# A transformer-like block on one core: three LayerNorms folded into weights and later scales, the sine product moved to VectorE, new orders

## The reference

```
ln(x)  = (x - mean(x)) / sqrt(var(x) + 1e-5)            # per row
1: q,k,v = ln(x) @ Wqkv.T ; q,k = elu(q)+1, elu(k)+1     # 16 heads of 8, linear attention
   x += ((q @ (k.T v)) / (q . sum(k) + 1e-6)) @ Wproj.T + bproj
2: y  = relu(ln(x) @ W_fc.T)**2 @ W_proj.T               # 128 -> 512 -> 128
   x += (spikes counted over 5 steps of mem = 0.9*mem + y - (mem>1)) / 5
3: Q,K,V = ln(x) @ Wq.T, Wk.T, Wv.T ; Q,K rotated by cos, sin of the row number
   x += softmax(Q K.T / sqrt(128), keys up to row+1) @ V
4: as 2, with the same weights
```

## Time and profile before

| what | value |
|---|---|
| median of 3 runs | 205.46 us (203.21 to 206.3) |
| the profiled execution | 205.26 us |
| its span, first to last instruction | 203.5 us |
| mean granted TensorE clock | 0.98 |
| busy: TensorE, VectorE, ScalarE, GpSimd | 180.9, 159.6, 114.2, 64.0 us |
| chain that ended last, by engine | TensorE 72%, VectorE 12%, issue 7%, ScalarE 3%, GpSimd 3% |

### The profile page before, as it was taken

One profiled execution on the slowest core, in us unless ns is written; L12 is line 12 of the kernel. 1 busy time (PEld: TensorE's weight loads), 2 busy tenths in 40 slices (PEclk: granted clock), 3 DMA queues, 4 the chain that ended last, 5 costly groups with the idle time before them and its releaser, 6 DMA issues.

```text
span 203.5 us, 3973 instructions
## 1 busy us (share of the span) xinstructions
PE 180.9 (89%) x1264; PEld 159.5 (78%) x1264; DVE 159.6 (78%) x495; ACT 114.2 (56%) x265; POOL 64.0 (31%) x86
## 2 busy tenths in 40 slices
PE   7389969799989989598969999799999999999971
PEld 2189948597787868586868999699999999999961
DVE  2995685999897999988998787955879663974895
ACT  2269831659649188287836786364064945574260
POOL 7760054353372834232752105400010213012110
PEclk9969996999999999999999999999999999999998
DMA  5980000000000030300000000000000001000111
GB/s 179 279 252 2 3 0 0 2 3 0 0 5 2 1 102 4 89 14 3 4 0 0 0 3 0 0 2 3 0 3 0 2 3 52 2 0 3 52 52 52
DMA packets 9825, 5.96 MB, mean 29 GB/s; under 512 B 447, under 2 KB 9422, under 8 KB 9806
## 3 DMA queue, kind: packets, MB, share of 16 engines
q1 hardware_dynamic: 9086, 5.25, 8.7%
q10 hardware_dynamic: 720, 0.47, 0.8%
HBM read 4.66 MB, written 1.05 MB: 28 GB/s over the span
## 4 chain that ended last, share of the span: by engine, by line
PE 72%; DVE 12%; issue 7%; ACT 3%; POOL 3%; DMA 1%; DVEq 0%; ACTq 0%; POOLq 0%
PE bank_o L1099 14%; PE bank_m L1026 10%; PE bank_p L1087 7%; PE bank_s L910 6%; PE bank_s L912 5%; PE bank_s L911 5%; PE bank_h L910 3%; DVE xn L712 3%; PE bank_h L912 3%; PE bank_h L911 3%; PE bank_m L927 3%; PE bank_p L1062 2%; PE bank_h L962 2%; POOL rstd L457 2%; DMA id_sb<-in_ident 1%
## 5 line engine op out<-in xcount | busy, mean ns | idle before, releaser
L1099 PE MATMUL bank_o<-vone,pt 128*128 128x128 f32 x272 | 35.7, 275 | 0.9 <-DVE pt L845 0.5
L1099 PEld LDWEIGHTS bank_o<-vone,pt 128*128 128x128 f32 x272 | 33.6, 191 | 2.3 <-DVE pt L845 0.9
L1026 PE MATMUL bank_m<-wd,hid 128*128 128x128 f32 x256 | 32.9, 276 | 1.0 <-ACT hid L623 1.0
L1026 PEld LDWEIGHTS bank_m<-wd,hid 128*128 128x128 f32 x256 | 31.1, 192 | 2.2 <-issue 1.4
L612 ACT ACTIVATE relu<-bank_h 128x512 f32<-128x512 f32 (+2 forms) x44 | 20.5, 483 | 15.6 <-PE bank_h L912 12.7
L450 POOL TENSOR_SCALAR veps<-mom 128x4 f32<-128x4 f32 (+2 forms) x19 | 4.4, 231 | 62.9 <-DVE mom L694 62.8
L499 POOL TENSOR_TENSOR hid<-relu 128x512 f32<-128x512 f32 (+2 forms) x14 | 12.4, 892 | 37.0 <-ACT relu L612 37.0
L672 ACT COPY pt<-bank_p 128x512 f32<-128x512 f32 (+3 forms) x25 | 13.2, 528 | 16.2 <-PE bank_p L1087 13.8
L794 DVE SCALAR_TENSOR_TENSOR spiked<-y,spiked 128x512 bf16<-128x512 f32 (+2 forms) x34 | 19.1, 562 | 0.6
L712 DVE TENSOR_SCALAR xn<-xs,mom,rstd 128x128 f32<-128x128 f32 x54 | 17.2, 377 | 3.0 <-POOL rstd L457 2.8
L457 POOL TENSOR_TENSOR rstd<-veps,mhalf 128x4 f32<-128x4 f32 (+2 forms) x19 | 18.4, 966 | 1.4 <-POOL veps L450 0.2
(11 more groups left out here) (137 smaller groups left out, 426.5 us busy)
## 6 DMA issues: line engine op xcount, KB each, us to landing
xs<-in_x SPq DMA_DIRECT2D x4, 256.0 KB, 5.2
cos_sb<-in_cos SPq DMA_DIRECT2D x4, 256.0 KB, 4.8
sin_sb<-in_sin SPq DMA_DIRECT2D x4, 256.0 KB, 5.2
out_x<-xs SPq DMA_DIRECT2D x3, 256.0 KB, 2.3
mask_sb<-in_mask SPq DMA_DIRECT2D x1, 320.0 KB, 8.3
...
```

Source lines behind the costliest of these rows:

```text
L1026: last = nc.tensor.matmul(MB[:, C * t:C * t + C], hid[:, j % 2, m, P * t:P * t + P], wd[:, m, :], start=(m == 0), stop=(m == M - 1))
L1099: last = nc.tensor.matmul(O[:, C * (i % TG):C * (i % TG) + C], pt[:, n % 3, P * b:P * b + P], v[:, k, :], start=(k == 0), stop=(k == i))
```

## The change

LayerNorms 2 to 4 (step index 1 to 3) no longer normalise the rows ahead of the product. Since a product with ln(x) equals rstd times the product of x with weights whose mean over the input channels has been taken off, the change does this:

- The weights W_fc and the rotary Wq, Wk, Wv are centred once: `centre` on GpSimd makes the identity minus 1/128, and the steps `centre-1` and `centre-2` on TensorE multiply it with the raw weights in full precision, 512 columns into H1 and 384 into MB. `w_hi-1`, `w_hi-2` (ScalarE) and `w_lo-1`, `w_lo-2` (both on VectorE now) read these banks; `w_hi-1` also copies the centred W_fc back to w_fc_sb.
- `turn-n-g` for n of 1 to 3 transposes the raw rows xs; it waits for the residual sum that made them (rows_ready) and not for `norm`. `norm-n-g` for these n and `nmr` are gone. `stats` and `rstd` stay.
- For LayerNorm 3 the rstd is applied to q, k and v when the bank is copied (`qkv_copy`: an activation with the scale taken from the table). For LayerNorms 2 and 4, relu and square carry the scale through as its square, so `rstd` holds 1 / (var + eps) there (power -1) and `y` applies it: one activation for each tile on ScalarE, or one product with a broadcast operand on VectorE.
- The sine product moves from GpSimd to VectorE; `rsin` and its use are the same.
- All four orders are new: which engine squares, copies and evacuates which piece changes, w_lo-0 comes after rstd-0-1 on GpSimd, kv-0-0 comes between the first two turns.

```diff
     "pe": """
+turn-0-0 kv-0-0 turn-0-1 kv-0-1 q-0 kv-1-0 kv-1-1 turn-0-2 q-1 acc-0 turn-0-3 kv-2-0 kv-2-1 q-2 kv-3-0 kv-3-1 acc-1
+q-3 acc-2 acc-3 centre-1 ao-0 centre-2 ao-1 at-0 pr-0 at-1 turn-1-0 ao-2 f1-0-0 turn-1-1 f1-0-1 pr-1 f1-0-2 f1-0-3
+at-2 f1-1-0 f1-1-1 f2-0-0 f2-0-1 pr-2 turn-1-2 f1-1-2 f1-1-3 ao-3 turn-1-3 f1-2-0 f1-2-1 f2-1-0 f1-2-2 f1-2-3 f2-1-1
...
+turn-3-4 pv-15-0 f2-8-0 f1-9-0 f2-8-1 f1-9-1 pt-15-3 pv-15-1 pv-15-2 pv-15-3 f1-9-2 f1-9-3 turn-3-5 f1-10-0 f1-10-1
 f2-9-0 f1-10-2 f1-10-3 f2-10-0
     "act": """
+q_exp-2 kv_exp-3-0 kv_exp-3-1 q_exp-3 w_hi-1 w_hi-2 aT_copy-0 hi-1-0 aT_copy-1 relu-0-0 hi-1-1 relu-0-1 sq-0-0 sq-0-1
...
     "dve": """
+heads-1 w_lo-2 x1-0 stats-1-0 lo-1-0 heads-2 lo-1-1 x1-1 sq-0-2 stats-1-1 stats-1-2 y-0 spike-0-0 spike-0-1 x1-2
     "pool": """
-vnext_zero ids rstd-0-0 w_lo-0 rstd-0-1 rstd-0-2 bias-0 rstd-0-3 w_lo-2 bias-1 bias-2 rstd-1-0 nmr-1-0 rstd-1-1 sq-0-1
+vnext_zero ids centre rstd-0-0 rstd-0-1 w_lo-0 rstd-0-2 bias-0 rstd-0-3 rstd-1-0 bias-1 bias-2 sq-1-1 rstd-1-1
...
+        def make_sin(eng, g):
+            eng.wait_ge(v_ready, TG * (g + 1))
+            eng.wait_ge(trig_in[g], 32)
+            if g:
+                eng.wait_ge(half_ready[0], g)
+                eng.wait_ge(half_ready[1], g)
+            eng.tensor_tensor(
+                rsin[:].rearrange("p t (a c) -> p t a c", a=2),
+                qk[:, g % 2].rearrange("p t (a c) -> p t a c", a=2),
+                sin_sb[:, g % 2].unsqueeze(2).to_broadcast([P, TG, 2, C]), ALU.mult).then_inc(*one(done["sin", g]))
+
+        def rows_ready(eng, n, g):
+            t0, nt = NORM_JOBS[n][g]
+            if n == 0:
+                eng.wait_ge(x_in[g], 16)
+            elif n == 1:
+                eng.wait_ge(x1_ready, (t0 + nt - 1) // TG + 1)
+            elif n == 2:
+                eng.wait_ge(xf_ready, next(k for k, (a, b) in enumerate(JOBS) if a + b >= t0 + nt) + 1)
+            else:
+                eng.wait_ge(x3_ready, t0 + nt)
...
-                    nc.gpsimd.tensor_tensor(rstd[:, n, ts], veps[:, n, ts], mhalf[:, 0:nt],
+                    nc.gpsimd.tensor_tensor(rstd[:, n, ts], veps[:, n, ts], (mone if n % 2 else mhalf)[:, 0:nt],
...
+                elif step[0] == "centre":
+                    pool.wait_ge(id_in, 16)
+                    nc.gpsimd.tensor_scalar(centre[:], id_sb[:], -1.0 / C, None, ALU.add).then_inc(centre_ready, 1)
...
+                        act.wait_ge(centred[k], 1)
+                        src = (None, H1, MB)[k][:, 0:n]
+                    if k == 1:
+                        nc.scalar.copy(w_fc_sb[:], src)
+                    nc.scalar.copy(wh[:, o:o + n], src).then_inc(w_hi, 1)
...
-                    nc.scalar.copy(y[:, j % 2, 0:width], MB[:, 0:width]).then_inc(*one(done["y", j]))
+                    n, g, scale = scale_of(j)
+                    act.wait_ge(rstd_ready[n], g + 1)
+                    for t in range(JOBS[j][1]):
+                        last = nc.scalar.activation(y[:, j % 2, P * t:P * t + P], MB[:, P * t:P * t + P], ACT.Copy,
+                                                    scale=scale[:, t:t + 1])
...
-                    nc.scalar.copy(qk[:, g % 2, t, :], bank[:, 0:2 * C])
-                    nc.scalar.copy(v[:, n, :], bank[:, 2 * C:3 * C]).then_inc(v_ready, 1)
+                    scale = rstd[:, 2, n:n + 1]
+                    nc.scalar.activation(qk[:, g % 2, t, :], bank[:, 0:2 * C], ACT.Copy, scale=scale)
+                    nc.scalar.activation(v[:, n, :], bank[:, 2 * C:3 * C], ACT.Copy, scale=scale).then_inc(v_ready, 1)
...
-                    nc.vector.tensor_copy(y[:, j % 2, 0:width], MB[:, 0:width]).then_inc(*one(done["y", j]))
+                    nc.vector.tensor_tensor(
+                        y[:, j % 2, 0:width].rearrange("p (t c) -> p t c", c=C),
+                        MB[:, 0:width].rearrange("p (t c) -> p t c", c=C),
+                        scale.unsqueeze(2).to_broadcast([P, JOBS[j][1], C]), ALU.mult).then_inc(*one(done["y", j]))
...
+                if step[0] == "centre":
+                    k = step[1]
+                    bank = (None, H1, MB)[k]
...
+                    nc.tensor.matmul(bank[:, 0:WEIGHTS[k][1]], centre[:], RAW[k], start=True, stop=True).then_inc(
+                        centred[k], 1)
...
-                    pe.wait_ge(*done["norm", n, g])
+                    if n == 0:
+                        pe.wait_ge(*done["norm", n, g])
+                    else:
+                        rows_ready(pe, n, g)
...
+                        last = nc.tensor.transpose(bank[:, C * t:C * t + C], xs[:, t0 + t, :] if n else xn[:, j % 2, t, :],
+                                                   id_sb[:])
```

More of the change, by code:

```diff
@@ new lines @@
+at-3 f1-3-0 f2-2-0 f2-2-1 f2-2-2 count-0 f2-2-3 count-1 pr-3 turn-2-0 f1-3-1 f1-3-2 turn-1-4 qkv-0-0 f1-3-3 qkv-0-1
+qkv-0-2 f1-4-0 qkv-0-3 f2-3-0 f2-3-1 f2-3-2 f2-3-3 count-2 f1-4-1 tqk-0-0 tqk-0-1 turn-2-1 f1-4-2 f1-4-3 s-0-0 s-1-0
+qkv-1-0 qkv-1-1 qkv-1-2 pt-0-0 qkv-1-3 f2-4-0 f2-4-1 pt-1-0 f2-4-2 f2-4-3 count-3 pv-0-0 s-2-0 tqk-1-0 tqk-1-1
+turn-2-2 pv-1-0 pt-2-0 s-3-0 s-3-1 pv-2-0 s-4-0 pt-3-0 s-4-1 s-5-0 pv-3-0 qkv-2-0 pt-4-0 turn-3-0 s-5-1 qkv-2-1
+count-4 qkv-2-2 qkv-2-3 pt-4-1 turn-2-3 pv-4-0 pv-4-1 f1-5-0 pt-5-0 pt-5-1 s-6-0 f1-5-1 s-6-1 tqk-2-0 tqk-2-1 pv-5-0
@@ L187 @@
+rstd-1-2 sq-1-2 sq-1-3 lo-1-3 bias-3 rstd-1-3 rstd-2-0 sq-3-1 sq-3-2 rstd-1-4 rstd-2-1 sq-4-2 lo-2-2 rstd-2-2 lo-3-0
+rstd-3-0 sq-5-3 rstd-2-3 rot-3-1 rstd-3-1 sq-6-1 sq-6-0 rstd-3-2 sq-8-2 rstd-3-3 rstd-3-4 sq-10-1 rstd-3-5
 """,
@@ L223, in hybrid_block @@
         rstd = sb("rstd", 4, T)
-        nmean = sb("nmean", 4, T)
-        nmr = sb("nmr", 4, T)
         mhalf = sb("mhalf", TG)
-        xn = [sb(f"xn{k}", 2, TG, C) for k in range(2)]
+        mone = sb("mone", TG)
+        xn = sb("xn", 2, TG, C)
+        centre = sb("centre", P)
         xh = [sb(f"xh{k}", 2, W, dt=F32R) for k in range(2)]
@@ L363, in one @@
             return signal[0], 1
-        def on_act_before(norm, g):
-            return sum(engine_of["norm", norm, k] == "act" for k in range(g))
         def raw_used(eng):
@@ L540, in _ @@
                 if step[0] == "w_hi":
-                    o, n = WEIGHTS[step[1]]
-                    act.wait_ge((wa_in, wf_in, wr_in)[step[1]], 16)
-                    nc.scalar.copy(wh[:, o:o + n], RAW[step[1]]).then_inc(w_hi, 1)
-                elif step[0] == "norm":
-                    n, g = step[1:3]
-                    lane, j = lane_job(n, g)
-                    t0, nt = NORM_JOBS[n][g]
-                    act.wait_ge(nmr_ready[n], on_act_before(n, g) + 1)
-                    if j >= 2:
-                        act.wait_ge(xT_ready[lane], j - 1)
-                    for t in range(nt):
-                        last = nc.scalar.activation(
-                            xn[lane][:, j % 2, t, :], xs[:, t0 + t, :], ACT.Identity,
-                            bias=nmr[:, n, t0 + t:t0 + t + 1], scale=rstd[:, n, t0 + t:t0 + t + 1])
-                    last.then_inc(*one(done["norm", n, g]))
+                    k = step[1]
+                    o, n = WEIGHTS[k]
+                    src = RAW[0]
+                    if k == 0:
+                        act.wait_ge(wa_in, 16)
+                    else:
[4 more added lines that the diff above has]
+                    nc.scalar.copy(wh[:, o:o + n], src).then_inc(w_hi, 1)
                 elif step[0] == "hi":
@@ L631, in _ @@
                         y_used(act, j - 2)
-                    nc.scalar.copy(y[:, j % 2, 0:width], MB[:, 0:width]).then_inc(*one(done["y", j]))
+                    n, g, scale = scale_of(j)
[3 more added lines that the diff above has]
+                                                    scale=scale[:, t:t + 1])
+                    last.then_inc(*one(done["y", j]))
                 elif step[0] == "sign":
@@ L919, in _ @@
             for step in plan["pe"]:
-                if step[0] == "turn":
+                if step[0] == "centre":
+                    k = step[1]
+                    bank = (None, H1, MB)[k]
+                    if k == 1:
+                        pe.wait_ge(centre_ready, 1)
+                    pe.wait_ge((wa_in, wf_in, wr_in)[k], 16)
+                    claim(bank)
+                    nc.tensor.matmul(bank[:, 0:WEIGHTS[k][1]], centre[:], RAW[k], start=True, stop=True).then_inc(
+                        centred[k], 1)
+                    reader[bank.name] = (w_lo[k], 1)
+                elif step[0] == "turn":
                     n, g = step[1:]
```

169 lines of the change are left out of this document (70 added, 99 removed).

## The result

The changed kernel took 193.99 us (median of 4 runs, 193.53 to 194.89) against 205.56 us for the kernel before beside it on the same chip: a ratio of 0.948 [0.939, 0.957]. A second measurement of the same kernel, put beside the later experiments, gave 193.14 us (192.18 to 194.37) and 0.943 [0.938, 0.948]. The forecast was 200.2 us with a range down to 195.5 us; the change gave 12 us where 5 were forecast. The profiled execution took 193.53 us, its span 191.4 us.

A forecast was written before the change was run, and what follows sets the result against it. TensorE, busy 180.9 us of a 203.5 us span, was taken as the bound, its 22.6 us idle nearly all there was to win. 205.26 - 3.1 (start, entry) - 3.3 (rotation, turns) + 1.3 (scales) = 200.2 us; range 195.5 to 205.3.

The forecast's parts named there:

- The entry: LayerNorm 2, 25 to 45 us: transposes need only raw rows; 2.4 us won there, lead 3.1 us including 0.7 from LayerNorm 1.
- the 0.57: Granted clock from 31 to 35 us before, stretching busy time by about 1.7 us; its absence afterwards would show the forecast right.
- The start: LayerNorm 1: moving the weights' low part behind the second reciprocal root gains 0.7 us, bounds 0 and 1.3 us.
- The centring products: Two full-precision products around ao-0 add 1.6 us to TensorE, costed at nothing beyond the entry's check.
- What is given back: TensorE waits for rotated and normalised tiles after 41 us: 60% of 5.5 us gained, 3.3 us; bounds 0 and 8.6 us.
- 1.3 us of scales: Scaled q, k, v and y copies on ScalarE cost TensorE 1.3 us; bounds 0 and 7 us.
- a sign of being right: Expected in the trace after: TensorE idle from 41 to 135 us near 6 us, busy total 180 to 181 us.
- everything that waits goes: Rival, chance 0.20: VectorE's relief of 10 us makes nearly all 8.6 us of TensorE idle vanish, giving 195 us.
- the rival of scaled copies as the bound: Rival, chance 0.12: ScalarE's scaled copies bound the kernel, 206.5 to 210.3 us; decides from 0.2 us for each of 32 copies.
- The sine: Four sines move from GpSimd to VectorE: 4.9 us added, about 5 us of blocking removed, most of TensorE's 4.4 us wait goes.
- The block from 140 us and the tail: TensorE's fully busy 140 to 190 us only moves forward; no tail gain, the saved chain being hidden; bounds -1 to +0.5 us.
- the forecast's 0.42: Chance of the main forecast, 198 to 202.5 us; 0.38 of it counted towards faster, under 201.35 us, in a total of 0.58.

The follow-up runs named there:

- the runs of the start: Changed kernel with the old orders up to the first attention's sums, run twice: 193.15 and 193.34 us; changed kernel beside them 193.14 us.
- fold_sine_old: Kernel before with centred weights, raw rows transposed, scales on the copies and sine on VectorE, but the old orders: 206.38 us, ratio 1.005.
- a_dead_norms: Changed kernel with 38 VectorE normalisations of LayerNorms 2 to 4 put back as work nobody reads: 201.33 us, ratio 0.985.
- a_plain: Changed kernel with plain ScalarE copies of q, k, v and y in place of the scaled ones: 193.93 us, ratio 0.947.

## Why the prediction was right or wrong

**The entry: right in place and nearly in size.** Forecast against trace: turn-1-0 at 32.2 and 33.3 us, f1-0-0 at 33.6 and 34.8, turn-1-2 at 41.0 and 41.5, the lead at 41 us 3.1 and 2.3; what is missing lies in the start, below. The granted clock was 1.00 from 25 to 41 us, the level of 2.4 GHz throughout; the 0.57 is gone.

**The start: wrong sign, and small.** I took 0.7 us of gain from w_lo-0's move. It came where I looked: the first four normalisations take 1.12 us for 1.78 us. But the new order has the next four later, beside the bias on GpSimd, and there the price returns, which I had not counted:

```profile
6.91 1.12 DVE L717 TENSOR_SCALAR xn<-xs,mom,rstd 128x128 f32<-128x128 f32 x4
...
10.07 2.18 DVE L717 TENSOR_SCALAR xn<-xs,mom,rstd 128x128 f32<-128x128 f32 x4
...
10.63 1.27 POOL L492 TENSOR_TENSOR xs<-xs,bias 128x512 f32<-128x512 f32 x1
```

The last sums (acc-3) start at 25.4 us where they started at 24.1; q-3 is now ahead of them and a centring product right behind. The wait for the head outputs, 1.35 us before, takes most of that up: the first residual sum starts at 32.56 us for 32.18 us. In the kernel's time none of it is seen, as the runs of the start show.

**The centring products: right.** Their printed lengths are 1.02 and 0.81 us, and the next products start 0.86 and 0.64 us behind theirs: 1.5 us against 1.6 us, ahead of a wait that covered most of it.

**What is given back: the failed step.** I took 60% of the 5.5 us that the list of waits names, set 1.3 us of scales against it, and called 8.6 us of idle the bound, so 2.0 us net from 41 to 140 us. Measured at equal work it is 8.9 us. The runs show four things that the step had wrong.

*The bound was no bound.* The idle of the busy column understates what TensorE can still take in. A matmul's record runs on past the start of the next where they are packed closely, so the same work shows less busy time when it is packed more closely: the 272 products of L1099 have a printed mean of 275 ns each and cover 35.7 us together, 131 ns each; after (L1127) they cover 34.9 us. At equal work the stretch went from 90.37 to 87.54 us of busy time, with the same weight loads, and 2.6 us of idle are still there beside the 8.9 us won. The busy total says the same: I had 180 to 181 us as a sign of being right, and it is 176.8 us, although the centring products were added. (That 8.9 us is more than 8.6 us proves nothing by itself, as the lead is good to about 1 us.) The Trainium skill's page "Perfetto Trace Analysis", section "Identifying the Most-Contended Engine", says that matmul busy time is not a good measure of how near a kernel is to its limit, and that weight-load busy time is better. This case agrees: from 41 to 140 us matmuls were busy 90.37 of 99 us, which looks 91% full, weight loads 78.67 us, which is 79%; they rose to 87.38 us; in the stretch after 140 us, where TensorE never waits, they stand at 37.86 of 40 us, 95%.

*VectorE's time was counted by the direct waits only.* That VectorE's relief makes nearly all of the idle vanish was in the text as a rival at 0.20 ("everything that waits goes", 195 us), and its time is what came; the idle from 41 to 140 us fell to 2.5 us, where I had named 6 us as a sign of being right. Its reason is only half of the matter: with the same relief the old orders gain nothing (fold_sine_old). In the new orders 11.8 us of normalisations cost 8.2 us when put back (a_dead_norms), nearly one for one up to 76 us.

*The scales cost nothing* (a_plain), where I had 1.3 us. The size of one was right, 94 ns for 128 columns and 104 ns for 256; the Trainium skill's "ScalarE: Activation LUTs", section "What ACT_TABLE_LOAD costs", gives about 93 ns for each pointer operand, which this case agrees with, now for a PSUM source too. Without the scales ScalarE was busy 4.8 us less. The 0.22 us of the upper bound was not seen, so the rival of scaled copies as the bound was far from its point of decision; only in the old orders did they cost 4.4 us.

*The orders were taken as a detail of carrying out the fold.* They are what turns it into time: 12.4 us between two kernels with the same steps, in part on other engines, 3.9 us ahead of turn-2-0 and 8.0 us behind it. What they do that can be read off: a turn stands right behind the sum that frees it; the products that wait for rotated tiles have other work ahead of them; the copies of q, k, v have theirs. That these places are what brings the time is my reading; which engine's order brings how much stays open, as they were not swapped one by one.

**The sine: right in mechanism, small in size.** I had it as part of the 3.3 us; it is worth 2.7 us in the kernel before, 1.3 us beside the fold in the old orders and 3.7 to 4.6 us in the new ones. "The move is free to VectorE" came as said: 4.9 us more, 5.3 us less. No wait for the rotated tiles, no small sum of 2.5 us: as said.

**The block from 140 us and the tail: right.** The lead is 11.2 us at 140 us and 11.1 us at the end; turn-3-5 starts at 182.4 us where it started at 194.2, 11.8 us earlier, the last down-projection f2-10-0 12.1 us. Nothing was won or lost there. The saved chain was hidden as said, which two rows of the timeline after show against the earlier trace rows:

```profile
179.06 2.84 PE L1127 MATMUL bank_o<-vone,pt 128*128 128x128 f32 x24
...
182.35 0.33 PE L954 MATMUL bank_m<-id_sb,xs 128*128 128x128 f32 x1
```

The transposes follow the last attention product by 0.45 us where 2.6 us lay between, filled with down- and up-projections of which most now come before.

The sum as it came: start and entry 2.3, 41 to 140 us 8.9, tail 0, together 11.2 us; the span is 12.1 us shorter, and the 0.9 us between the two is within what the count of matmul work can tell.

**The chances.** For "faster" I took 0.38 out of the forecast's 0.42 and called it most of its lower two thirds; two thirds of 0.42 are 0.28, so by its own words the chance of "faster" should have been under 0.5.
